# Last layer's routing and gathering in pieces within the attention's loop, a sum moved to PE, the result stored in four parts

## The reference

```python
# attention of the last layer: 16 heads of 8; own keys (128) and context keys (77)
p = softmax(q k^T * scale);  pa = softmax(q ka^T * scale)
out = (p v) * (1 - sigmoid(g)) + (pa va) * sigmoid(g);  x += tanh * (out @ Wo + bo)
# feed-forward of the last layer: t = 32 experts, 4 sets, tokens in groups of 32
grouped = layernorm(x).reshape(B, g, t, d)
logits = einsum('bgtd,des->bgtes', grouped, controller) + tie
perm = (logits == max(logits, axis=-3, keepdims=True))
dispatched = einsum('bgtd,bgtes->bgesd', grouped, perm)
inner = relu(einsum('bgesd,desf->bgesf', dispatched, f1) + bias)
intermediate = einsum('bgesf,esfd->bgesd', inner, f2)
out = einsum('bgesd,bgtes->bgtd', intermediate, perm)
```

## Time and profile before

| what | us |
|---|---|
| three runs: median (lowest, highest) | 711.68 (710.56, 713.01) |
| profiled execution: own time | 705.82 |
| its span, first to last instruction | 703.9 |
| last attention update to first expert matmul | 33.52 |
| from there to the last update of X | 32.22 |
| store of the result | 4.30 |
| busy over the span: PE, DVE, ACT, POOL | 600.0, 442.5, 317.5, 212.0 |

### The profile page before, as it was taken

The page is one execution under the profiler, slowest core; times in us unless marked ns, Lnnn a source line. Parts: engine busy times, 40 slices in busy tenths (PEclk is TensorE's granted clock), DMA queues, the critical chain, the costliest instruction groups (busy, mean ns, idle before and its releaser), DMA issues.

```text
span 703.9 us, 14703 instructions
## 1 busy us (share of the span) xinstructions
PE 600.0 (85%) x5691; PEld 395.1 (56%) x5691; DVE 442.5 (63%) x1250; ACT 317.5 (45%) x706; POOL 212.0 (30%) x412
## 2 busy tenths in 40 slices
PE   4999999999997998456898799899988888875687
PEld 4666666666655695323564455544555555553474
DVE  4377777868786215779888676356566666417542
ACT  2435363635433351746433122115667676731344
POOL 2123334263455256500213334312351511102000
PEclk9999999999999899778699899999999899955899
DMA  9780000000002252000001503022030210003001
GB/s 290 177 268 1 1 1 1 1 9 8 1 16 80 71 158 79 1 0 2 0 1 37 123 2 104 1 73 54 5 102 6 58 51 6 7 1 120 2 4 61
DMA packets 33751, 34.94 MB, mean 50 GB/s; under 512 B 8746, under 2 KB 29522, under 8 KB 33106
## 3 DMA queue, kind: packets, MB, share of 16 engines
q1 hardware_dynamic: 31216, 31.41, 15.5%
q0 software_dynamic: 1024, 2.11, 0.9%
q10 hardware_dynamic: 1442, 0.48, 0.3%
HBM read 20.02 MB, written 5.26 MB: 36 GB/s over the span
## 4 chain that ended last, share of the span: by engine, by line
PE 66%; DVE 15%; issue 6%; ACT 6%; POOL 5%; DMA 2%; DVEq 0%; POOLq 0%; ACTq 0%; SPq 0%
PE bank L2007 5%; PE bank L594 5%; PE bank L1716 5%; PE bank L518 4%; PE bank L2022 4%; PE bank L550 4%; PE bank L527 4%; PE bank L447 3%; PE bank L1775 3%; PE bank L2055 3%; POOL y_tokens L1234 2%; PE bank L537 2%; PE bank L562 2%; PE bank L1290 2%; DVE mx L2158 1%
## 5 line engine op out<-in xcount | busy, mean ns | idle before, releaser
L2158 DVE TENSOR_REDUCE mx<-bank 128x4 f32<-128x512 f32 (+1 forms) x128 | 72.0, 582 | 44.4 <-PE bank L2015 43.3
L2226 ACT ACTIVATE area_a<-bank 128x512 f32<-128x512 f32 (+1 forms) x128 | 74.0, 596 | 45.2 <-PE bank L2022 43.8
L949 ACT ACTIVATE area_a<-bank,beta 128x154 f32<-128x154 f32 x128 | 41.9, 411 | 74.5 <-PE bank L518 74.4
L1037 POOL TENSOR_TENSOR area_a<-area_a,rs 128x512 f32<-128x512 f32 (+1 forms) x48 | 40.8, 879 | 50.6 <-DVE rs L753 50.6
L447 PE MATMUL bank<-ones_b 128*128 128x512 bf16 x154 | 48.4, 412 | 1.7 <-DVE X L1875 0.9
L594 PEld LDWEIGHTS bank<-area_a 128*128 128x128 f32 x320 | 39.5, 191 | 18.4 <-ACT area_a L942 9.7
L594 PE MATMUL bank<-area_a 128*128 128x128 f32 x320 | 46.4, 285 | 0.0
L518 PE MATMUL bank<-ctx_flat,area_a 128*128 128x154 f32 x256 | 42.2, 300 | 0.1
L550 PE MATMUL bank<-area_a,xnT 128*128 128x512 f32 (+1 forms) x96 | 41.7, 515 | 0.0
L518 PEld LDWEIGHTS bank<-ctx_flat,area_a 128*128 128x128 f32 x256 | 37.0, 193 | 7.9 <-issue 7.3
L1716 PE MATMUL bank<-area_a 128*128 128x512 f32 x80 | 40.7, 637 | 0.0
(11 more groups left out here) (359 smaller groups left out, 1459.3 us busy)
## 6 DMA issues: line engine op xcount, KB each, us to landing
area_a<-xn_area SPq DMA_DIRECT2D x48, 128.0 KB, 2.5
area_b<-in_w SPq DMA_DIRECT2D x16, 256.0 KB, 4.8
f<-in_f SPq DMA_DIRECT2D x1, 2048.0 KB
area_a<-in_f SPq DMA_DIRECT2D x1, 2048.0 KB, 8.0
area_b<-xn_area SPq DMA_DIRECT2D x6, 308.0 KB, 5.5
area_a<-in_rows SPq DMA_DIRECT2D x10, 128.0 KB, 2.8
x_slots<-xn_area SPq DMA_DIRECT2D x1, 1032.0 KB, 7.9
area_a<-x_slots SPq DMA_DIRECT2D x8, 129.0 KB, 2.3
```

Of the source, the lines that this page charges most:

```text
L949: m = act.activation(kk0[:, g % 2, h, :], src[:, (h - lo) * 2 * T:(h - lo + 1) * 2 * T], ACT.Identity, bias=beta0[:, h:h + 1])
L1037: pool.tensor_tensor(e, e, rs0[:, b % 2, lo:hi].unsqueeze(2).to_broadcast([128, hi - lo, SLOTS0[c][1] - SLOTS0[c][0]]), ALU.mult).then_inc ...
L2158: dve.tensor_reduce(mx3[:, b % 2, aux, heads3(half, 1 - odd)], SCORES_RING3[j % 2][:, 0:4 * n].rearrange("p (h k) -> p h k", k=n), AX.X, A ...
L2226: act.activation((ea3 if aux else em3)[:, heads3(half, odd), :], EXP_RING3[j % 2][0:T if aux else 128, :].rearrange("p (h q) -> p h q", q= ...
```

## The change

Routing and gathering of groups 0, 1 and 2 move into the attention's loop, each step at one place (b, j) of the order of an engine; group 3 stays behind it, with filler matmuls. In the loop, statistics and norms go tile by tile, and the choices of groups 0 and 1 in six pieces of half the width. The gathers of groups 0 and 1 go strip by strip, four matmuls a round, through the two banks that the scores have left; group 2's is whole, in turn 16. DVE's add of the two streams goes: PE sums them by two matmuls with the identity, accumulated. d3 gets another place and order (four runs of 16 columns for each expert), f1 is loaded in two parts, and the result is stored in four parts.

```diff
+OUT_PARTS = ((0, 6), (6, 11), (11, 14), (14, 16))
...
+        d3 = carve("A", ([10760], (4, 2080)), 128)[:, :, 0:2048].rearrange("p i (e n) -> p i e n", e=ES3)
+        D3_PLACE = (2, 3, 0, 1)
+        F1_EARLY = 48
...
+        def tensor_gather3(pe, g, rounds, first_bank):
+            for j in range(4):
+                for r in rounds:
+                    p = slice(G3 * r, G3 * r + G3)
+                    m = pe.matmul(D_BANK[first_bank + r - rounds[0]][:, j::4], xn4[p, g % 2, j, :], pt3[p, g % 2, j, :],
+                                  start=True, stop=True)
+            m.then_inc(d3_in_psum, 1)
+
+        def tensor_gather_round3(pe, g, r):
+            if r == 0:
+                pe.wait_ge(pt3_done, g + 1)
+                if g == 0:
+                    pe.wait_ge(max3_done, 8 * B)
+            at_least(pe, d3_dve_done, 4 * g + r - 1)
+            tensor_gather3(pe, g, (r,), 2 + r % 2)
...
+        def tensor_ahead3(pe, b, j):
+            if (b, j) == (9, 4):
+                tensor_norms_turned3(pe, 0)
+            if (b, j) == (10, 1):
+                pe.wait_ge(late_loaded, LATE_LOADS * 16)
+                tensor_expert_logits3(pe, 0)
+            if (b, j) == (11, 5):
+                tensor_norms_turned3(pe, 1)
+            if (b, j) == (12, 0):
+                tensor_expert_logits3(pe, 1)
+            if (b, j) == (13, 0):
+                tensor_choice_turned3(pe, 0)
+            if (b, j) == (13, 4):
+                tensor_choice_turned3(pe, 1)
+            if b == 14 and j < 6:
+                tensor_gather_round3(pe, j // 4, j % 4)
+            if b == 15 and j < 2:
+                tensor_gather_round3(pe, 1, 2 + j)
+            if (b, j) == (15, 2):
+                tensor_norms_turned3(pe, 2)
+            if (b, j) == (15, 4):
+                tensor_expert_logits3(pe, 2)
+            if (b, j) == (15, 7):
+                tensor_choice_turned3(pe, 2)
+            if (b, j) == (16, 1):
+                tensor_gather_whole3(pe, 2)
...
-                pe.transpose(OT3, o3[:, :], ident[:, :]).then_inc(oT3_in_psum, 1)
+                for aux in range(2):
+                    m = pe.matmul(OT3, ov3[:, aux, :, :].rearrange("p h d -> p (h d)"), ident[:, :], start=(aux == 0), stop=(aux == 1))
+                m.then_inc(oT3_in_psum, 1)
...
+        def vector_ahead3(dve, b, j):
+            if b in (6, 9, 13):
+                g = (6, 9, 13).index(b)
+                if j == 0:
+                    dve.wait_ge(x_updated, 6 * B + 4 * g + 4)
+                if j < 4:
+                    vector_tile_stats3(dve, g, j)
+                elif j < 6:
+                    vector_tile_moments3(dve, g, 2 * j - 8)
+                    vector_tile_moments3(dve, g, 2 * j - 7)
+            if b == 8 and j >= 4:
+                vector_tile_norm3(dve, 0, j - 4)
+            if b == 11 and j < 4:
+                vector_tile_norm3(dve, 1, j)
...
+            if b in (10, 12) and (b, j) not in ((10, 1), (10, 0), (12, 0), (12, 7)):
+                n = j - (2 if b == 10 else 1)
+                vector_choose3(dve, (b - 10) // 2, n % 3, n // 3 * 2, n // 3 * 2 + 2)
+            if b == 14 and 1 <= j < 7:
+                vector_gathered_round3(dve, (j - 1) // 4, (j - 1) % 4)
+            if (b, j) == (14, 6):
+                for u in range(4):
+                    vector_tile_norm3(dve, 2, u)
+            if b == 15 and 1 <= j < 3:
+                vector_gathered_round3(dve, 1, j + 1)
+            if (b, j) == (15, 5):
+                for step in range(3):
+                    vector_choose3(dve, 2, step)
+                dve.wait_ge(x_updated, 6 * B + 14)
+                vector_tile_stats3(dve, 3, 0)
+                vector_tile_stats3(dve, 3, 1)
+            if (b, j) == (16, 1):
+                dve.wait_ge(x_updated, 6 * B + 15)
+                vector_tile_stats3(dve, 3, 2)
+                for u in range(3):
+                    vector_tile_moments3(dve, 3, u)
+                vector_gathered_whole3(dve, 2)
...
-                dve.tensor_tensor(o3[:, :], ov3[:, 0, :, :].rearrange("p h d -> p (h d)"), ov3[:, 1, :, :].rearrange("p h d -> p (h d)"),
-                                  ALU.add).then_inc(o3_done, 1)
+                m.then_inc(o3_done, 1)
...
+        def scalar_ahead3(act, b, j):
+            if (b, j) == (9, 6):
+                scalar_g_xnT(act, 16, PREP3)
+            if (b, j) == (11, 7):
+                scalar_g_xnT(act, 17, PREP3)
+            if (b, j) == (13, 2):
+                scalar_choice3(act, 0)
+            if (b, j) == (13, 6):
+                scalar_choice3(act, 1)
+            if (b, j) == (15, 3):
+                scalar_g_xnT(act, 18, PREP3)
+            if (b, j) == (15, 7):
+                scalar_choice3(act, 2)
+            if (b, j) == (16, 2):
+                scalar_gathered3(act, 2)
...
+                if b in (11, 15):
+                    gpsimd_g_rstd(pool, 21 if b == 11 else 22)
                 split_maxima(b)
+                if b == 8:
+                    gpsimd_g_rstd(pool, 20)
...
         def tensor_moe3(pe):
+            keep_busy(pe, bank[6], 10)
+            tensor_norms_turned3(pe, 3)
+            tensor_expert_logits3(pe, 3)
+            keep_busy(pe, bank[6], 5)
+            tensor_choice_turned3(pe, 3)
+            keep_busy(pe, bank[6], 1)
+            tensor_gather_whole3(pe, 3)
+            keep_busy(pe, bank[6], 2)
...
+                sp.wait_ge(sT3_in_psum, 8 * 12)
+                sp.dma_start(f1_early, t["f1_3"][:, 0:F1_EARLY, :]).then_inc(f1_loaded, 16)
+                sp.wait_ge(sT3_in_psum, 8 * B)
+                sp.dma_start(f1_late, t["f1_3"][:, F1_EARLY:ES3, :]).then_inc(f1_loaded, 16)
+            for lo, hi in OUT_PARTS:
+                sp.wait_ge(x_updated, 16 * (LAST_STAGE - 1) + hi)
+                sp.dma_start(t["out"][:, lo:hi, :], X[:, lo:hi, :]).then_inc(out_stored, 16)
+            sp.wait_ge(out_stored, 16 * len(OUT_PARTS))
```

More of the change, by code:

```diff
@@ L1999, in tensor_prep3, with tensor_norms_turned3, tensor_expert_logits3 @@
             m.then_inc(prep3_in_psum, 1)
+        D_BANK = bank[0:4]
+        def tensor_norms_turned3(pe, g):
+            if g == 0:
+                pe.wait_ge(prep3_done, block3(3, V3))
+            elif g == 1:
+                pe.wait_ge(perm3_done, 1)
+            else:
+                pe.wait_ge(pt3_done, g)
+            tensor_g_xnT(pe, g + 16, PREP3)
+        def tensor_expert_logits3(pe, g):
+            pe.wait_ge(g_xnT_done, g + 17)
+            pe.matmul(PREP3[:, :], ctrl3[:, :], xnT4[:, g % 2, :], start=True, stop=True).then_inc(l3_in_psum, 1)
@@ new lines, in tensor_choice_turned3 @@
+        def tensor_choice_turned3(pe, g):
+            pe.wait_ge(perm3_done, max(g + 1, 2))
+            at_least(pe, pt3_done, g)
+            for j in range(4):
+                tok = (4 * g + j) * 128
+                m = pe.transpose(PREP3[:, j * 128:(j + 1) * 128], perm3[:, tok:tok + 128], ident[:, :])
+            m.then_inc(pt3_in_psum, 1)
+        def tensor_gather3(pe, g, rounds, first_bank):
+            for j in range(4):
+                for r in rounds:
[3 more added lines that the diff above has]
+            m.then_inc(d3_in_psum, 1)
@@ L2391, in tensor_moe3, with f1 @@
         def tensor_moe3(pe):
[L2392 to L2422, removed]
+            keep_busy(pe, bank[6], 10)
[6 more added lines that the diff above has]
+            keep_busy(pe, bank[6], 2)
+            pe.wait_ge(f1_loaded, 2 * 16)
+            pe.wait_ge(d3_act_done, 4)
+            pe.wait_ge(d3_dve_done, 12)
+            def f1(es):
+                return f1_early[:, es, :] if es < F1_EARLY else f1_late[:, es - F1_EARLY, :]
             def first(r):
@@ L2427, in first @@
                         es = 8 * (SETS3 * r + s_) + e % 8
[L2428 to L2429 removed]
+                        out = IN_BANK[r][F3 * s_:F3 * s_ + F3, (e % 8) * NG3:(e % 8 + 1) * NG3].rearrange("p (i n) -> p i n", i=4)
+                        m = pe.matmul(out, f1(es), d3[:, :, es, :], start=True, stop=True)
                 m.then_inc(in3_in_psum, 1)
@@ L2529, in scalar_moe3 @@
         def scalar_moe3(act):
[L2530 to L2539 removed]
+            scalar_g_xnT(act, 19, PREP3)
+            scalar_choice3(act, 3)
+            scalar_gathered3(act, 3)
             def relu(r):
@@ L2563, in gpsimd_moe3 @@
         def gpsimd_moe3(pool):
-            for k in range(20, 24):
-                gpsimd_g_rstd(pool, k)
+            gpsimd_g_rstd(pool, 23)
         @block.sync
```

124 lines of the change are left out of this document (73 added, 51 removed).

## The result

The changed kernel takes 703.95 us, the median of 20 runs (699.94 to 710.98), against 711.23 for the kernel before in as many runs on the same chips. The ratio is 0.9906, with a 95% interval of 0.9883 to 0.9929: faster by 7.3 us, a small gain but clear of the noise, where 18.7 were forecast. Some executions are slower than the rest whatever the kernel, so every ratio here is taken from the fast executions alone and need not be the quotient of the medians. The profiled execution took 703.78 us, its span is 702.0. The kernel before was profiled in an execution of 705.82 us, 5.4 under its median here, so the two profiles differ by 2.0 us only; no trace shows where those 5.4 us lie.

A forecast was written before the change was run, and what follows sets the result against it. No engine was taken as full: three engines hand rings over, then a 33.52 us chain of small steps follows. Terms -21.5 +5.0 -0.3 -1.9 +4.3 +0 -0.8 -2.9 +0.6 -1.2 = -18.7 turn 711.7 into 693, range 686 to 701.

The forecast's parts named there:

- turn 16: Last attention turn: full clock in place of 0.50 saves 2.0 us, DVE's gather copies cost some 0.1; together -1.9 us.
- Turn 14's +5.0: Turn 14: six gather rounds of 1.1 us each, less 1.6 us hidden in PE's waits, add 5.0 us.
- turn 15's -0.3: Turn 15: at full clock, with two rounds, transposes and logits added, 10.3 us against 10.57 before.
- rival 5: Turns 14 and 15: clock falls to 0.5 since a round feeds 32 of 128 rows; +17 us, whole 715; chance 0.04.
- the rival's further 4.7: Behind the attention: clock stays low in turn 16 (2.0 us) and routing (2.7 us); as a rival alone 698, chance 0.13.
- Routing -21.5: Stretch behind the attention: only group 3 is left, 12.0 us instead of 33.5, saving 21.5 us.
- A gather round 1.1: Turns 14 and 15: four fp32 matmuls on one strip take 1.1 us, bounds 0.3 and 1.09.
- POOL's rstd +0.6: Turn 7: group 0's rstd (1.3 us) ahead of POOL's splits delays the next split of maxima, half covered; +0.6 us.
- PE's sum 0: All 16 turns: PE's two matmuls replace DVE's add and one transpose at no net cost, bounds -1.6 and +1.6 us.
- the stall of turn 7: DVE's add, stretched to 1.12 us under POOL, goes: -0.8 us, and -2.9 us of clock loss in turns 7 and 8.
- Turns 6 to 13 as a whole: Moved statistics, norms, choices, logits and transposes add 4.3 us (bounds 0 and about 9), before the stall, clock and rstd terms.
- Store -1.2: End of kernel: last store has 128 KB instead of 1024, 2.8 us against 3.9 to landing; -1.2 us.

The follow-up runs named there:

- a quarter of the gathers: Changed kernel with each single-strip gather round issuing one of its four matmuls, copies and waits kept; 695.58 us, ratio 0.9782 to the kernel before.
- three strips: Changed kernel with gathers of groups 0 and 1 three strips side by side, third bank, all in turn 14; 686.83 us, 0.964 to the kernel before.
- four fillers: Changed kernel with four filler matmuls (128 rows, 512 columns) behind each of the eight gather rounds; 697.59 us, ratio 0.9829 to the kernel before.
- the kernel before with fillers: Kernel before with two full-height filler matmuls at the head of every step of turns 14 and 15, no gathers there; 715.07 us, ratio 1.0061.
- PE's sum alone: Kernel before with only the two-matmul sum of the streams in place of DVE's add and one transpose; 714.33 us, ratio 0.9985.
- the filler of 32 rows: Changed kernel with one 32-row filler behind each gather round: 703.73 us, 0.9811 to the kernel before; its twin with 128 rows: 707.07 us, 0.9938.

## Why the prediction was wrong

**The step that failed** is the sentence behind turn 16: "I take the full clock because turns 14 and 15 are now packed." Turn 14's +5.0 and turn 15's -0.3 rest on it, and rival 5, which names the place and, with the narrow rounds, part of the mechanism, got 0.04 with the reason "the rounds fill exactly those waits". Filling waits was taken for keeping the clock. The runs show otherwise: PE fully busy at half clock (changed kernel, a quarter of the gathers), PE busy 10.06 of 11.34 at full clock (three strips), PE fully busy at full clock (four fillers; the kernel before with fillers). So the share of time that PE is busy does not decide alone; what it is fed counts. Waits count too: without its fillers the routing stage, PE busy 6.37 of 14.71 us, ran at 0.51. The price was 14.1 us by four fillers' turns, somewhat under the rival's 17, and the rival's further 4.7 for a low clock behind the attention did not come: turn 16 ran at 1.00 and the routing stage at 0.88. The rounds themselves are not shown to have brought the fall: with PE's sum alone and no gather it came 2.8 us into turn 14, in the changed kernel 2.4.

**Luck in the number.** The 5.86 us between profile and median were carried over unchanged; in the changed kernel they were 0.17. Against the profiled execution the forecast missed by 16.7 us (687.1, measured 703.8), against the median only by 11.

The Trainium skill (TensorE: Matmul & The Clock Gate, Part 1) says that the gate is set by how busy PE has been. By that rule turns 14 and 15, busy for 37.78 us on end, would run at 2.4 GHz; the measurement (0.55 and 0.65 on average, 0.50 for 19.87 us of turn 14) decides against it here.

**The rows had it.** Before, turn 14 was *busier* than the steady turns, 6.58 of 7.68 against 6.84 of 8.39, and yet the clock fell right behind it, in a turn with 9.30 of 10.57 busy. The difference to turn 13 was not the share but the missing plain scores. Read so, rival 5 deserved far more than 0.04.

**The other steps.**
- Routing -21.5: right, -20.9. The last gather took 1.92 us and not 1.22, part of the way at half clock (0.88 over the stage); the fillers hold most of it.
- A gather round 1.1: measured 1.15 at full clock. Turn 14 without its fillers is 13.3, not 12.7: 0.1 a round. The drain of the Trainium skill (TensorEngine Tiling, Key Properties), which the prediction put at 0.2 a round by the row of 64-row scores, would be 1.2 for these six; 0.6 is all there is, from whatever cause. The row itself is a wait of the weight load, not of the matmuls.
- Turn 16: 6.33, not 5.6, at clock 1.00 as forecast. The two copies of the gather hold up DVE for 1.03 us and stand in the chain; they were costed at 0.1.
- POOL's rstd +0.6: mis-sized. Turn 8 took 10.39, not 9.1; one turn later the rstd costs nothing and turn 8 takes 9.12, so the term was 1.25. PE waited 1.22 us for POOL's split of the maxima:

```profile
560.89 0.23 PE L2124 MATMUL bank<-ident_b,mcol 128*128 128x128 bf16 x1 [1.22 <-POOL mcol L2506]
```

  That half of it is covered was wrong: the split came late by all of it.
- PE's sum 0 and the stall of turn 7: steady turns 8.44 in place of 8.39, turn 7 1.04 less, turn 8 2.55 less by the sum alone. Right in place and size (-3.7 forecast for stall and clock, -3.6 measured, in one execution of each; the kernel before with fillers, the same up to turn 13, took 10.79 us in turn 7 and not 9.48, so the size differs by the execution). But the forecast did not see that the clock then falls earlier in turn 14. The Trainium skill (SBUF — State Buffer, Who interferes with whom) says that a DVE instruction with two SBUF inputs contends with a GpSimd instruction that reads SBUF; the trace agrees in that the add alone was stretched, 1.12 and 0.60 us against 0.29, and the products that read PSUM were 0.49 for two in all these turns, in the changed kernel right under a two-input operation of POOL:

```profile
553.12 1.15 POOL L2460 TENSOR_TENSOR xn_area<-tmp,xn_area 128x512 bf16<-128x512 f32 x1
...
553.29 0.49 DVE L2334 TENSOR_TENSOR ov<-bank,rs 128x128 f32<-128x128 f32 x2
```

- Turns 6 to 13 as a whole: forecast +4.3 - 0.8 - 2.9 + 0.6 = +1.2; measured 74.30 against 73.57, +0.7, with rstd's 1.25 in it. Turns 10 and 12 took 9.08 and 9.67, inside the 9 to 9.7 named.
- Store -1.2: -2.0. The last 128 KB land in 1.8 us, under the 2.8 read from a load of that size.
- Experts: not in the sum; 31.10 at 1.00 against 32.22 at 0.95. With other kernels 31.1 to 39.5 were seen for the same 704 matmuls, at mean clocks from 1.00 down to 0.74.
- The chances named for faster add up to 0.94, not 0.93.

## What to carry to other kernels

When you pack work into PE's waits, ask what the added work feeds, not how long it takes: in a stretch where only narrow matmuls are left (32 or 64 rows, 32 columns), more of them can leave PE busy all the time at half clock and cost more than the waits. Issue the strips of an array side by side: one, two, three and four strips of 32 rows took 1.15, 1.16, 1.17 and 1.15 us, and three at a time, with a third bank, turned a gain of 7 us into one of 26. And look at the turns in which the clock is already low before, and at what they lack, before you put anything there.

## What the hardware showed that was not expected

- PE busy without a gap for some 31 us (614.3 to 645.5) at a granted clock of 0.50 to 0.52, in 64-row bf16, 32-column and 32-row fp32 matmuls; and full clock again at about 645 without any pause before; what came just ahead was full-height, four and eight fp32 transposes of 128 by 128 (below). Eight such transposes at 619.61 did not bring it back, so this is a hint and no more. What exactly the chip weighs (rows, columns, or their product) is not settled by these runs: the filler of 32 rows did no worse than that of 128.

```profile
641.34 1.11 PE L1294 MATMUL bank<-ident,xn 128*128 128x128 f32 x4
...
642.92 1.97 PE L2131 MATMUL bank<-ident,area_a 128*128 128x128 f32 x8
```

- What is won on the clock in one place is not sure to be kept: PE's sum won 3.6 us in turns 7 and 8, and 6.0 went in turns 14 to 16, in the one execution that was profiled; its runs as a whole show no difference.
- Eight us more work took less time: turns 14 and 15 with four fillers a round took 32.02 us, without them 37.78.
